# Expert weights held stationary and streamed tile by tile, attention key blocks taken in pairs, in a fused image-attention-expert kernel

## The reference

```python
h = image_transformer(x)                       # conv patches, 2 layers of linear attention, (4, 256, 192)
h = concatenate([h, txt], axis=1)              # (4, 384, 192) -> 1536 tokens of 192
h = h + attn(layernorm(h))                     # below
h = h + experts(layernorm(h))                  # below

# attn: 12 heads of 16 channels over all 1536 tokens, keys = queries, normalised
q = (hs @ Wq.T + bq) per head;  q = q / max(norm(q), 1e-12);  v = hs @ Wv.T + bv
sim = -(AA - 2.0 * q @ q.T + AA.T) * HD ** (-0.5)
out = softmax(sim) @ v

# experts: top 4 of 16 for each token
t = rmsnorm(x, norm_scale)
g = t @ gate_w.T + gate_b;  top_vals, top_idx = top_k(g, 4);  route_w = softmax(top_vals)
h = t @ mlp1_w[e].T + mlp1_b[e]                # 192 -> 768, for the chosen experts
a = swiglu(h)                                  # min(glu, 7) * sigmoid(1.702 glu) * (clip(lin, -7, 7) + 1)
y = a @ mlp2_w[e].T + mlp2_b[e]                # 384 -> 192
out = x + sum(y * route_w)
```

## Time and profile before

| | before |
|---|---|
| median of 3 runs | 792.63 us (792.56 to 793.79) |
| the profiled execution | 790.85 us, its span 789.1 us |
| busy in the span | PE 88%, ACT 49%, DVE 55%, POOL 44% |
| PE busy, 250 to 436 us | 180.82 us of 186 |
| PE busy, 512 to 767 us | 254.20 us of 255 |
| granted TensorE clock | 0.99 to 1.00 in both stretches, 0.57 from 475 to 503 us |

### The profile page before, as it was taken

The page is one execution under the profiler, slowest core; times in us unless marked ns, Lnnn a source line. Parts: engine busy times, 40 slices in busy tenths (PEclk is TensorE's granted clock), DMA queues, the critical chain, the costliest instruction groups (busy, mean ns, idle before and its releaser), DMA issues.

```text
span 789.1 us, 15394 instructions
## 1 busy us (share of the span) xinstructions
PE 695.0 (88%) x4250; PEld 416.3 (53%) x4251; DVE 434.6 (55%) x1275; ACT 389.8 (49%) x784; POOL 347.8 (44%) x403
## 2 busy tenths in 40 slices
PE   4588989788867999999999995699999999999990
PEld 4557786578632222222222223377777777777760
DVE  0153757675672577777666644355555555555540
ACT  0032436533313999899989891134434344343430
POOL 4121223222230255555555444156666666666661
PEclk9798999999995999999999996599999999999995
DMA  9999980000014122322222200233323333233324
GB/s 275 411 389 320 321 274 1 1 1 1 21 55 108 61 55 104 98 91 100 63 82 103 103 24 22 79 68 52 52 43 51 52 52 52 43 51 52 52 31 70
DMA packets 31140, 76.60 MB, mean 97 GB/s; under 512 B 4335, under 2 KB 24672, under 8 KB 28672
## 3 DMA queue, kind: packets, MB, share of 16 engines
q1 hardware_dynamic: 17156, 59.50, 24.1%
q0 software_dynamic: 12400, 15.50, 9.8%
q10 hardware_dynamic: 1552, 1.18, 0.5%
HBM read 59.49 MB, written 40.11 MB: 126 GB/s over the span
## 4 chain that ended last, share of the span: by engine, by line
PE 72%; DVE 9%; DMA 4%; POOL 4%; ACT 4%; issue 3%; SPq 1%; ACTq 0%; DVEq 0%; POOLq 0%
PE ps L815 13%; PE ps L946 11%; PE ps L947 11%; PE ps L802 9%; PE ps L965 8%; PE ps L656 3%; DMA big<-patches 3%; PE ps L956 3%; ACT mid L1073 2%; POOL rstd L443 2%; PE ps L732 1%; DVE stat L1165 1%; DVE mid L1173 1%; PE ps L742 1%; PE ps L629 1%
## 5 line engine op out<-in xcount | busy, mean ns | idle before, releaser
L1073 ACT ACTIVATE mid<-ps 128x1536 f32<-128x1536 f32 x144 | 200.1, 1457 | 27.1 <-PE ps L802 27.1
L815 PE MATMUL ps<-mid 128*32 128x384 f32 x1152 | 123.6, 502 | 3.4 <-POOL mid L491 2.0
L566 POOL TENSOR_TENSOR mid<-mid 128x384 f32<-128x384 f32 x63 | 62.5, 991 | 99.8 <-PE ps L956 78.0
L946 PE MATMUL ps<-big,mid 128*128 x252 | 104.6, 497 | 0.3 <-issue 0.3
L947 PE MATMUL ps<-big,mid 65*128 x252 | 104.0, 493 | 0.0
L802 PE MATMUL ps<-mid 52*128 52x512 f16 x432 | 88.3, 389 | 6.2 <-ACT mid L1073 5.6
L965 PEld LDWEIGHTS ps<-big,mid 128*128 128x128 f32 x378 | 64.6, 189 | 18.4 <-issue 2.0
L965 PE MATMUL ps<-big,mid 128*128 x378 | 71.9, 326 | 1.5 <-DVE mid L1509 1.5
L1501 DVE TENSOR_SCALAR mid<-ps 128x384 f32<-128x384 f32 x63 | 35.1, 558 | 68.6 <-PE ps L947 68.6
L517 POOL DMA_INDIRECT expert_in<-t_row,slot_u x48 | 47.9, 999 | 46.0 <-DVE slot_u L1391 35.0
L1115 ACT ACTIVATE mid<-ps,mid 128x192 f32<-128x192 f32 x63 | 26.6, 422 | 84.3 <-PE ps L965 81.4
(11 more groups left out here) (224 smaller groups left out, 1192.7 us busy)
## 6 DMA issues: line engine op xcount, KB each, us to landing
expert_in<-expert_in SPq DMA_DIRECT2D x16, 1358.5 KB, 36.4
mid<-expert_in SPq DMA_DIRECT2D x63, 104.5 KB, 2.1
big<-patches SPq DMA_DIRECT2D x3, 2048.0 KB, 32.0
big<-w_a SPq DMA_DIRECT2D x4, 1536.0 KB
big<-w SPq DMA_DIRECT2D x4, 1152.0 KB
big<-w_b SPq DMA_DIRECT2D x4, 780.0 KB
big<-patches SPq DMA_DIRECT2D x4, 512.0 KB, 7.5
expert_in<-zero_rows POOLq DMA_DIRECT2D x1, 1567.5 KB, 16.2
```

Source lines behind the costliest of these rows:

```text
L566: nc.gpsimd.tensor_tensor(actv[r], prod[r], sig[r], ALU.mult).then_inc(actv_ready, 1)
L815: last = nc.tensor.matmul(oacc[32 * g:32 * g + 32, 0:QW], vhead[par][:, kb, :], probs[kb % 3][:, g * QW:(g + 1) * QW], start=(kb == 0), st ...
L946: nc.tensor.matmul(o, xtT[r][:, 0:P], w1a_sb[:, bass.ds(ex * 768 + half * FF, FF)], start=True, stop=False)
L1073: nc.scalar.activation(probs[kb % 3], SETS[kb % 2], ACT.Exp, scale=0.5).then_inc(probs_ready, 1)
```

## The change

Four things change.

1. **Expert weights stationary.** `w1` no longer lies in SBUF. For every tile SP loads the expert's weights into one of `NW` = 4 sets of buffers: one transfer of 128 x 768 and two of 64 x 384 (the last 64 input channels, for the glu half at partitions 0 to 63 and for the lin half at 64 to 127), when `h_done` of tile j-4 has come. `mlp1` has them stationary and the transposed rows moving: six matmuls of 128 x 128 x 128, and six of contraction 64, alternately at rows 0 and 64 of the array. The result comes out transposed, so that `act_transpose` and `actT_copy` are gone and `mlp2` reads `actv` directly. The rows carry their last 64 channels twice (`RW` 209 to 273), and the bias, now one number per partition, is added in DVE's `clip` (three instructions of 128 columns for each half). The biases are loaded after the values of the attention (`v_in`), and turned on PE before head 0.
2. **Key blocks in pairs.** `weighted` of two blocks follows `scores` of two blocks, and the small jobs stand between them. There are four buffers `probs`.
3. **DVE's order in a head.** `prep` is cut in `prep_keys` (up to `aa`) and `prep_rest`; `prep_keys` stands ahead of `choose`, `prep_rest` behind `place`. `norm_stats`, `norm_square` and `norm_rows` each stand one place ahead of the stack copy that they followed.
4. SP does weight loads for the first two tiles ahead of its wait for the scatters.

The core of the diff:

```diff
+            sp.wait_ge(v_in, 16 * NB)
+            sp.dma_start(b1_rows, w1_b[CB:CB + 1, :].rearrange("o (k c) -> (o k) c", c=P)).then_inc(b1_in, 16)
...
+            def load_weights(j, q):
+                if not isinstance(j, int) or j >= NW:
+                    sp.wait_ge(h_done, j * 2 - (2 * NW - 2))
+                ex = sp.value_load(ej_i[0:1, bass.ds(j, 1)], min_val=0, max_val=E - 1)
+                sp.dma_start(w1_t[q], w1_a[:, bass.ds(ex * 768, 768)]).then_inc(w1_in[q], 16)
+                for half in range(2):
+                    sp.dma_start(w1_h[q][HROW * half:HROW * half + CB, :],
+                                 w1_b[0:CB, bass.ds(ex * 768 + half * FF, FF)]).then_inc(w1_in[q], 16)
...
+            load_weights(0, 0)
+            load_weights(1, 1)
+            sp.wait_ge(rows_out, 16 * (TOPK * NT + 1))
+            load_rows(0, 0)
...
+                for half in range(2):
+                    for c in range(3):
+                        nc.tensor.matmul(banks[half][:, c * P:(c + 1) * P], w1_t[q][:, half * FF + c * P:half * FF + (c + 1) * P],
+                                         xtT[r][:, 0:P], start=(c == 0), stop=False)
+                for c in range(3):
+                    for half in range(2):
+                        rows_ = slice(HROW * half, HROW * half + CB)
+                        last = nc.tensor.matmul(banks[half][:, c * P:(c + 1) * P], w1_h[q][rows_, c * P:(c + 1) * P],
+                                                xtT[r][rows_, P:2 * P], start=False, stop=(c == 2),
+                                                tile_position=(HROW * half, 0))
...
+                for kb in range(0, KEYB, 2):
+                    ahead(kb + 2)
...
+                        if kb == 2: out_transpose(r, base)
+                        if not last:
+                            if kb == 4: stacks(0, n + 1, base + 1)
+                            if kb == 8: stacks(1, n + 1, base + 2)
+                    ahead(kb + 3)
+                    if not first and kb == 10:
+                        logits(base + (2 if last else 4))
                     weighted(n, par, kb)
+                    weighted(n, par, kb + 1)
+                    if not first:
+                        if kb == 8: t_transpose(r, 1 - par, base + (1 if last else 3))
+                        if kb == 10: ranks(r, base + (3 if last else 5))
...
             scores(0, 1, None)
+            pe.wait_ge(b1_in, 16)
+            nc.tensor.transpose(b7[:, 0:E * 6], b1_rows, ident[0:E * 6, 0:E * 6]).then_inc(b1_psum, 1)
             pe_head(0, None, 0, True, False)
```

More of the change, by code:

```diff
@@ L42 @@
 NSPARE = MT - TOPK * NT
[L43 to L45 removed]
+COMB = C + CB
+TOKEN = COMB + E
+RW = TOKEN + 1
+NW = 4
+HROW = P // 2
 DUMP = NT * P
@@ L852, in pe_head, with ahead @@
                 base = 2 if first else tr_base(r)
-                for kb in range(KEYB):
-                    if kb + 2 < KEYB:
-                        scores(par, kb + 2, n * KEYB + (kb + 1))
+                def ahead(kb):
+                    if kb < KEYB:
+                        scores(par, kb, n * KEYB + (kb - 1))
                     elif not last:
-                        if kb + 2 == KEYB:
+                        if kb == KEYB:
                             pe.wait_ge(tr_taken, base + (2 if first else 3))
-                        scores(1 - par, kb + 2 - KEYB, n * KEYB + (kb + 1))
-                    weighted(n, par, kb)
[L862 to L871, removed]
-                    else:
-                        if kb == 1: out_transpose(r, base)
-                        if kb == 7: t_transpose(r, 1 - par, base + 1)
-                        if kb == 8: logits(base + 2)
-                        if kb == 10: ranks(r, base + 3)
@@ L950, in act_transpose, with mlp1 @@
-            def act_transpose(j, r, wait=True):
+                nc.tensor.transpose(o[:, P:2 * P], xt[r][:, P:2 * P], ident[:]).then_inc(x_read, 1)
+            def mlp1(j, q, n_loaded):
+                r = q % 2
+                pe.wait_ge(xT_ready, j + 1)
+                pe.wait_ge(w1_in[q], n_loaded)
+                if not isinstance(j, int) or j >= 2:
+                    pe.wait_ge(lin_ready, j - 1)
+                banks = [bank(1 + 2 * half + r) for half in range(2)]
+                for half in range(2):
[8 more added lines that the diff above has]
+                                                tile_position=(HROW * half, 0))
+                        if c == 2:
+                            last.then_inc(h_done, 1)
@@ L1010, in _ @@
+            x_transpose(0, 0, 16)
+            for j in range(NW):
+                tile_work(j, j, 0)
+            with pe.Fori(1, MT // NW) as i:
+                for q in range(NW):
+                    tile_work(i * NW + q, q, i * 16)
+            for j in range(MT // NW * NW, MT):
+                tile_work(j, j % NW, j // NW * 16)
+            mlp2(MT - 2, (MT - 2) % 2)
+            mlp2(MT - 1, (MT - 1) % 2)
         @block.scalar
@@ L1433, in dve_head @@
                     prep_squares(n + 2)
-                if not last and prep2:
                     prep(n + 2)
```

211 lines of the change are left out of this document (89 added, 122 removed).

## The result

| | before | changed |
|---|---|---|
| median | 793.21 us (792.56 to 794.16, 4 runs) | 799.47 us (798.01 to 803.26, 4 runs) |
| ratio | | 1.0088 [1.0056, 1.012] |
| the profiled execution | 790.85 us, span 789.1 | 803.26 us, span 801.5 |

The forecast was 766 us in a range of 742 to 788.

What follows compares the result with a forecast made beforehand. PE was taken to bound attention and expert stage. Expert tiles -43.4, attention +14.3, expert start +2.1 and end +0.3 make -26.7 from 790.85: 764.2, plus 1.8 for the median, so 766 us, range 742 to 788.

Steps and rivals of the forecast that it cites:

- SP's budget of a tile: Expert stage: SP's two row loads' worth and two more issues take 3.1 to 3.3 us, fitting in a 3.41 us tile.
- the second rival: Expert stage: the new bytes, or SP needing 0.5 us more, make the tile 3.8 us; 788 us in all, chance 0.15.
- The other half, the bytes: Expert stage: new weight bytes at 246 GB/s take 2.5 us, all bytes 3.8 a tile; the main forecast took 3.2, hidden.
- The gap on PE: Expert tile: sign of 3.8 us tiles with gaps ahead of the first `mlp1` matmul, named for a DMA.
- the first row load: Start of expert stage: two weight sets, 3.9 us together, ahead of SP's first row load cost 2.1 us.
- The tile on PE: Expert tile: 0.22 + 1.34 + 0.10 + 0.67 + 0.10 + 0.98 = 3.41 us of PE work, against 4.11 before.
- The first rival: Expert tile: half-height matmuls don't run side by side, so a tile takes 4.08 us; 807 us in all, chance 0.18.
- What the tiles give: Expert stage: each tile 0.70 us shorter, over 62 tiles 43.4 us gained.
- The head: Attention: the loop of small jobs sums to 20.19 us a head against 18.93, 1.26 more, 10.1 over eight heads.
- one sign that I named: Attention: PE idles about 1.3 us before the second stacks, waiting for DVE.
- The sum of attention: Attention: 2.4 for head 0, 2.6 for head 1, 10.1 for eight heads, -0.3 and -0.5: 14.3 us more.
- The third rival: Attention: the small jobs' loop is hidden and PE's 17.5 us bounds the head; 742 us in all, chance 0.15.

Runs made afterwards that it cites:

- e1: The changed kernel with the three weight loads of a tile made one of 128 x 1152, same bytes: 780.95 us, ratio 0.9865.
- e2: The changed kernel with the same three weight loads, the large one bringing 128 of its 768 columns: 799.3 us, ratio 1.0082.
- e10: Kernel e5 with two weight loads a tile, 128 x 768 and 128 x 384, for the one: 767.53 us, ratio 0.9685.
- e3: The changed kernel with all of `prep` behind `place` as before, nothing else undone: 794.23 us, ratio 1.0019.
- e4: The changed kernel with the old order of attention on PE, ACT and DVE: 789.37 us, ratio 0.9953.
- e11: Kernel e5 with the biases turned ahead of head 0, as in the changed kernel: 773.92 us, ratio 0.9736.
- e5: The changed kernel with one weight load a tile, the old attention order, and biases turned behind key block 2 of head 0: 770.28 us, ratio 0.9767.
- e8: Kernel e5 with rows of 209 numbers, the last 64 channels copied per tile by one more matmul: 796.84 us, ratio 1.0098.
- e12: The kernel before with one edit, `prep_keys` between `tT_copy` and `choose`, `prep_rest` behind `place`: 815.74 us, ratio 1.0271.

## Why the prediction was wrong

- **The step that failed is SP's budget of a tile**: "two more issues of about 0.38 (0.34 and a gap), 3.1 in all, and up to 3.3 with the waits and branches. It just fits." Measured is 3.88. A half-height load takes 0.48 us to issue, and I took the issue of a full-height row load for it: the two are 1.23 for my 0.76. The register work ahead of the row load and of the large load is 0.91 and 1.05 for 0.81 each. That makes 0.5 and 0.3 of the 0.8 us that I was short. e1 and e2 show that this, and nothing of the bytes, set the tile. It is the second rival, in its half that spoke of SP "0.5 more than I count"; it was 0.8, and so the tile is 3.93 and not that rival's 3.8. The other half, the bytes, is refuted by e2; they took 0.86 of 3.93, 3.4 us a tile, for my 3.2. The gap on PE stands ahead of `x_transpose`, for the row load, and not ahead of `mlp1`, as I had written. The same queue work made the first row load late: 3.6 us to the first tile for my 2.1.
- **The tile on PE** is 3.60 for 3.41. The full passes were right (1.43 for 1.34 and a change of form), the half-height ones take 0.87 for 0.77, `mlp2` 1.08 for 0.98. The first rival (4.08) is out: the halves do run side by side. (One reading behind this was off without harm: the 16 of `weighted` in the earlier trace rows are eight matmuls of two passes of 384 columns, not 16 matmuls. One after the other, at the 0.32 of such a pass, they would take over 5 us as well.) Where SP is out of the way (e1, e10), most tiles take 3.60.
- **What the tiles give** is therefore 62 x (4.11 - 3.93) = 11 us and not 43. These 32 us are most of the miss; the rest is 2.7 us in attention and 1.5 us ahead of the first tile.
- **The head** was right to a hundredth: 20.20 for 20.19. Link by link, from the rows above: `mask` to residual 8.89 (354.10 to 362.99) for 8.88; residual to `ms` 2.99, as forecast; the second stack copy to 367.15, then stacks, `scores` and the two `weighted` as forecast; `t_transpose` to the end of `tT_copy` 0.95; `prep_keys` and `choose` to the end of `mask` 3.72 for 3.75. But one sign that I named did not show: no idle time ahead of the second stacks. It stands two `scores` earlier, for ACT (0.90). The `scores` ahead of the second stacks end where the second stack copy does (367.23 and 367.15), so the way over `scores` and exponentials is as long as this part of the loop; that is read from these rows and not tried by itself. That I had not seen. And `prep_keys` taken away alone gives 1.0 us and not its 2.11, since 1.03 of it lies beside DVE's wait for `logits` (e3).
- **The sum of attention** was 14.3, and it is 17.0 in this execution: 3.8 by the first `weighted` for my 2.4, and 13.2 behind it for 11.9. In head 0 I left out that the `scores` of blocks 2 and 3 stand behind the bias wait too, and that PE works on at a granted clock of 0.56. Three heads (20.85, 21.59 and 21.30) have a clock of 0.92 and hold some 3.1 us in all over the 20.2 of the others.
- **The third rival** is out: none of the eight heads came near 17.5.
- **What stays open.** Heads of the old order took 19.25 (e4), 19.14 (e11) and 19.13 (e10), but 18.92 in e5 and e8, though e5 and e10 differ only in the expert stage. The place of the bias wait doesn't explain it (e10 has it late, too), nor do the wide rows alone (e5 has them). The traces show where it begins: DVE copies the first stacks 0.04 us behind PE's last transpose in the kernel before, in e5 and in e8, but 1.0 to 1.3 us behind it in e4, e10 and e11, and the profile names nothing that it waits for in between. PE's transposes and DVE's copy behind them, first in e5, where they end at 367.11, then in e4, where they end at 373.69:

```profile
366.60 0.51 PE L647 MATMUL ps<-ident,mid 128*128 128x128 f16 x6
...
367.14 1.11 DVE L1236 COPY mid<-ps 52x768 f16<-52x768 f16 x2 [1.07 <-PE ps L647]
```

```profile
373.18 0.51 PE L649 MATMUL ps<-ident,mid 128*128 128x128 f16 x6
...
374.97 1.11 DVE L1237 COPY mid<-ps 52x768 f16<-52x768 f16 x2 [2.31 <-PE ps L649]
```

  e5 and e8 ran on one chip, e4, e10 and e11 on the two others, and the kernel before is 2.7 us faster on the first. So the chip may be it; no kernel of the old order has traces from two chips. It is 2 to 3 us of a run, and its cause stays open.

The predicted 766 us is where the three mended versions lie (767.5 to 773.9), but that is by chance: those have the old attention, and a tile of 3.65 to 3.73 for my 3.41.

## What to carry to other kernels

Where a change moves data from resident to streamed, write the issuing queue's round out by its own rows before the bytes: here four issues (three for weights, one for rows) and two register reads of 3.88 us outweighed a PE tile of 3.60, and laying the weights out so that one full-height load brings them was worth 2.2%. Work that idles in a slack-rich place of an engine is not free at another: find the loop that the moved piece joins, and every result that it waits for there (e12). A link taken out of a loop gives back only what no other wait covers (e3). And a gap on PE costs twice where the clock falls behind it, so waits of one to six us are to be priced with what PE does next.

## What the runs showed of the hardware

- Two fp32 matmuls of contraction 64 at rows 0 and 64 ran side by side: twelve passes of 128 columns took 0.87 us when the two rows alternated in program order, 1.19 when three matmuls at one row followed three at the other and only the passes next to the border overlapped, and 1.43 at full height.
- The issue of a load of 64 partitions held SP's queue 0.48 us (1536 bytes a partition), that of 128 partitions 0.34 (3072) and 0.33 (1536, in e10).
- DMA's share of 0.86 at 210 GB/s did not bound the stage: in e2 it fell to 0.57 and the time stayed.
